# Masked attention with layer norm on one core: the layer norm's steps reordered on VectorE and GpSimd

## What is computed

```python
q = x @ Wq.T; k = x @ Wk.T; v = x @ Wv.T
rel = adj.T * (q @ k.T)                 # 1024 x 1024, mask of zeros and ones
rel = rel / norm(rel, axis=2)           # over the last axis, without the batch
y = x + rel @ v
out = (y - mean(y)) / sqrt(var(y) + 1e-5)
```

## Time and profile before

| | |
|---|---|
| median of 3 runs | 2031.97 us (2030.19 to 2032.34) |
| the profiled execution's own time | 2032.82 us |
| its span, first to last instruction | 2030.8 us |
| busy: PE, DVE, ACT, POOL | 97%, 75%, 35%, 47% |
| granted TensorE clock, mean | 0.994 of full speed |

### The profile page before, as it was taken

The page is one execution under the profiler, slowest core; times in us unless marked ns, Lnnn a source line. Parts: engine busy times, 40 slices in busy tenths (PEclk is TensorE's granted clock), DMA queues, the critical chain, the costliest instruction groups (busy, mean ns, idle before and its releaser), DMA issues.

```text
span 2030.8 us, 28664 instructions
## 1 busy us (share of the span) xinstructions
PE 1960.9 (97%) x9840; PEld 1667.5 (82%) x9840; DVE 1523.6 (75%) x2339; ACT 709.3 (35%) x1032; POOL 944.9 (47%) x640
## 2 busy tenths in 40 slices
PE   7799999999999999999999999999999999999998
PEld 5688878888787887878878788887888878788787
DVE  7587777877778777786877768777787777867776
ACT  5242424334243342323423234242433423334231
POOL 6543447344363443645534464343734436344352
PEclk8899999999999999999999999999999999999999
DMA  6534333344342434334352333543334434343411
GB/s 209 216 151 181 146 116 142 128 170 155 124 155 114 176 139 155 119 129 160 139 191 101 132 139 150 181 153 107 149 127 169 152 124 155 117 172 139 159 52 62
DMA packets 80414, 292.21 MB, mean 144 GB/s; under 512 B 7440, under 2 KB 7440, under 8 KB 76304
## 3 DMA queue, kind: packets, MB, share of 16 engines
q1 hardware_dynamic: 80400, 292.06, 39.0%
HBM read 251.13 MB, written 40.89 MB: 144 GB/s over the span
## 4 chain that ended last, share of the span: by engine, by line
PE 50%; issue 26%; POOL 17%; DVE 5%; DMA 1%; ACT 1%; POOLq 0%; DVEq 0%; SPq 0%; ACTq 0%
PE banks L410 17%; PE banks L412 17%; PE banks L411 17%; POOL square_sum L1057 8%; POOL scr L995 2%; POOL scr L987 2%; DVE x_lo L720 2%; POOL rstd L1074 2%; POOL rel L1050 1%; DMA w_kept<-v_raw 1%; POOL rnorm L1070 1%; DVE yv L887 1%; DVE stats L915 1%; DVE res L912 1%; DVE rel L823 1%
## 5 line engine op out<-in xcount | busy, mean ns | idle before, releaser
L410 PE MATMUL banks<-yv 128*128 128x512 f32 x1024 | 402.1, 393 | 38.9 <-DVE yv L887 38.9
L411 PE MATMUL banks<-yv 128*128 128x512 f32 x1024 | 399.0, 390 | 0.0
L412 PE MATMUL banks<-yv 128*128 128x512 f32 x1024 | 398.5, 389 | 0.0
L1057 POOL TENSOR_TENSOR square_sum<-square_sum,squares 128x512 f32<-128x512 f32 x224 | 319.8, 1428 | 87.2 <-ACT squares L639 76.6
L410 PE MATMUL banks<-yv,x_hi 128*128 128x512 f32 x896 | 349.7, 390 | 10.7 <-ACT rel L627 10.7
L411 PE MATMUL banks<-yv,x_hi 128*128 128x512 f32 x896 | 349.5, 390 | 0.0
L412 PE MATMUL banks<-yv,x_lo 128*128 128x512 f32 x896 | 349.5, 390 | 0.0
L1074 POOL TENSOR_TENSOR rstd<-var_eps,minus_half 128x1 f32<-128x1 f32 x128 | 130.4, 1018 | 316.0 <-DVE var_eps L919 316.0
L410 PEld LDWEIGHTS banks<-yv 128*128 128x128 f32 x1024 | 192.2, 188 | 90.4 <-DVE yv L887 51.6
L412 PE MATMUL banks<-aw,x_lo 128*128 128x256 f32 x896 | 253.6, 283 | 0.0
L411 PE MATMUL banks<-aw,x_hi 128*128 128x256 f32 x896 | 253.6, 283 | 0.0
(11 more groups left out here) (99 smaller groups left out, 3557.5 us busy)
## 6 DMA issues: line engine op xcount, KB each, us to landing
scr<-adj SPq DMA_DIRECT2D x128, 512.0 KB, 5.8
aw<-w_kept SPq DMA_DIRECT2D x16, 3584.0 KB, 11.0
aw<-a_kept SPq DMA_DIRECT2D x15, 3584.0 KB, 10.9
scr<-xT SPq DMA_DIRECT2D x32, 1024.0 KB, 7.1
res<-x SPq DMA_DIRECT2D x128, 256.0 KB, 2.7
out<-res SPq DMA_DIRECT2D x128, 256.0 KB, 2.0
a_kept<-aw SPq DMA_DIRECT2D x1, 3584.0 KB, 16.1
w_kept<-v_raw SPq DMA_DIRECT2D x3, 512.0 KB, 16.8
```

The source lines that it names most:

```text
L410: pe.matmul(bank_ap, l_hi, r_hi, start=first and i == 0, stop=False, skip_group_check=on)
L411: pe.matmul(bank_ap, l_hi, r_lo, start=False, stop=False, skip_group_check=on)
L412: mm = pe.matmul(bank_ap, l_lo, r_hi, start=False, stop=i == len(pairs) - 1, skip_group_check=on)
L1057: pool.tensor_tensor(square_sum[:, h, :], square_sum[:, h, :], squares[:, n % SQRING, :], ALU.add).then_inc(square_added, 1)
```

## The change

The reference to pieces by tile becomes a table, X_IN_TILE. On ScalarE the order of the instructions is the same as before (the loop is only written otherwise). On VectorE the x splits that belong to tile t+1 now stand behind the chunk's split in turn t, and ahead of `normalise(b, t)`; before, they stood behind it. Those of tile 0 still stand ahead of `output(b, 0)`. On GpSimd the power of tile t now stands ahead of the sum, and one sum follows each of the first four powers: power 0, S1, power 1, S3, power 2, S2, power 3, S4, powers 4 to 7. The last batch is as before. SP's and TensorE's programs are as before.

```diff
+        X_IN_TILE = {0: (X22,), 1: (X11, X12), 2: (S1,), 3: (S3,), 4: (S2,), 5: (S4,)}
...
                 norms(b)
                 for t in range(MT):
-                    if not last:
-                        for q in {0: (X22,), 1: (X11, X12), 2: (S1,), 3: (S3,), 4: (S2,), 5: (S4,)}.get(t, ()):
+                    if t == 0 and not last:
+                        for q in X_IN_TILE[0]:
                             x_piece(b + 1, q)
                     output(b, t)
                     if t + CRING < MT:
                         chunk(b, t + CRING)
+                    if not last:
+                        for q in X_IN_TILE.get(t + 1, ()):
+                            x_piece(b + 1, q)
                     normalise(b, t)
...
                 power_norm(b)
-                if not last:
-                    x_sum_of(b + 1, S1)
-                    x_sum_of(b + 1, S3)
-                power_var(b, 0)
-                if not last:
-                    x_sum_of(b + 1, S2)
-                power_var(b, 1)
-                if not last:
-                    x_sum_of(b + 1, S4)
-                for t in range(2, MT):
+                sums = {} if last else {0: (S1,), 1: (S3,), 2: (S2,), 3: (S4,)}
+                for t in range(MT):
                     power_var(b, t)
+                    for q in sums.get(t, ()):
+                        x_sum_of(b + 1, q)
```

More of the change, by code:

```diff
@@ L698, in batch @@
                         v_hi_piece(b, block, i)
+                if not last:
+                    for q in X_IN_TILE[0]:
+                        x_piece(b + 1, q)
                 for t in range(MT):
-                    if not last:
-                        for q in {0: (X22,), 1: (X11, X12), 2: (S1,), 3: (S3,), 4: (S2,), 5: (S4,)}.get(t, ()):
-                            x_piece(b + 1, q)
                     if t + CRING < MT:
                         chunk(b, t + CRING)
+                    if not last:
+                        for q in X_IN_TILE.get(t + 1, ()):
+                            x_piece(b + 1, q)
             y_first(0)
```

## The result

The changed kernel takes 2039.87 us (median of 6 runs, 2038.13 to 2040.39), the kernel before 2032.15 us beside it. The ratio is 1.0038, interval 1.0025 to 1.0051: slower by 7.7 us (0.4%), a quarter of the 29.7 us forecast.

What follows compares the result with a forecast made beforehand. TensorE, busy 97%, was taken as the bound, its waits for VectorE's chunk splits the winnable part. Later splits add 1.98 us a batch, 15 batches +29.7 us, to 2032.8: 2062.5 us, range 2048 to 2080.

Steps and rivals of the forecast that it cites:

- sign: Whole kernel: slower, by 29.7 us; slower was given 0.81, faster 0.15, no change 0.04.
- place: TensorE waits for VectorE's chunk splits at tiles 4 to 7, 0.34 us late, then 1.47 each.
- main mechanism: Each of four sums on GpSimd goes in ahead of VectorE's norm step and costs VectorE a full 2.26 us.
- the order of turns: VectorE and GpSimd: neither keeps its place from one instruction to the next; the one that stood goes in.
- the power's hold: Behind the chunk's split, VectorE's x split stands 0.40 us for GpSimd's power, four times a batch.
- the pace: VectorE, tiles 1 to 3: 7.02 us from chunk split to chunk split, against TensorE's 5.44.
- TensorE's waits: TensorE waits for the chunk's split 60 times, tiles 4 to 7, some 4.1 us of listed idle a batch.
- First rival: The norm step goes in ahead of the sum, no tile waits: faster, 1986 us; chance 0.15.
- second: Rival: only three of four sums hold VectorE, about 2029 us, next to no change; chance 0.04.
- third: Rival: the chunk's split stands too, or lateness reaches the next batch's products: 2078 us and up; chance 0.06.
- The rest: ScalarE's waits for sums, SP's later stores, x for tiles 5 to 7 and later line 775, costed at nothing.

Runs made afterwards that it cites:

- experiment 1: The kernel before with only GpSimd's order taken from the changed kernel (each sum right behind a power): 2068.74 us, ratio 1.0183.
- experiment 3: The changed kernel with each sum for the next batch cut to 2 of 512 columns, same instructions and waits: 1983.41 us, ratio 0.9767.
- experiment 4: The changed kernel with one wait more, GpSimd's sum after power t waiting for norm step t: 1983.80 us, ratio 0.9765.
- experiment 6: The changed kernel with each of the four sums split into two instructions of 512 columns: 1985.17 us, ratio 0.9764.
- experiment 2: The changed kernel with GpSimd's old order, so VectorE's part of the change alone: 2042.71 us, ratio 1.0054.
- experiment 7: The changed kernel with a tile's power over 8 columns in place of 1, the other 7 unused: 2059.2 us in one run.

## Why the prediction was wrong

- **Its sign, its place and its main mechanism were right.** Sums go in ahead of norm steps of 2.62 us (forecast 2.64) in tiles 1 to 3, X12's split stands for S1, and lines 912 to 919 run after the sum where they could have run beside it. Experiments 1, 3, 4 and 6 show it by four different times, each within 3 us of the time or range expected before it ran (1, 4 and 6 by the order of turns, 3 by the sums' length alone). Those expectations were written with the result and its trace at hand, and so with a power that holds nothing.
- **The term that failed is the power's hold**, in the prediction "the x split that is next on VectorE stands those 0.40 us. The wait is renamed, and I count its gain as nothing". The trace after, experiment 2's pace of 4.57 us and experiment 7 show that it stands for 0. With 1.22 - 0.08 in place of 0.40 + 1.08 the pace is 7.02 - 0.34 = 6.68 (measured 6.64), and tile 0 is 0.34 shorter too. Four times that is 1.4 us a batch, with 0.04 more in each of three tiles 1.5: 22 of the 22.6 us between forecast and result. The term counts four times a batch, and the forecast effect, 1.98 us a batch, was itself the difference between four sums' hold and what VectorE had lost and had in slack before; so this small term was three quarters of it.
- **What led to it:** from the power's row I knew when it ended after the chunk's split, 0.40, and read that as the time that it holds the ports. The row shows the first and not the second, and "splits and norm steps on VectorE never run together with a sum or a power" went beyond the rows: for a power they had only the power itself standing. No row of before had an instruction of VectorE standing behind a power, so the hold was unknown from 0 to 0.40, 24 us in all; I named that bound and took half of it into the range. In full it would have been 2062.5 - 24 = 2038.5, 1.4 us from the result.
- **TensorE's waits:** forecast 60, tiles 4 to 7; they were 45. At tile 4 the chunk was in time by then but for 0.1 us, which is the same 0.34 again.
- **First rival** (1986, the norm step ahead): it didn't happen by itself, but its price was right; experiment 4 brings it about and takes 1983.8. The second and third had no part.
- **The rest held.** ScalarE, the stores, x of the later tiles and line 775 cost nothing: in the list of waits after, TensorE has none that repeats but the 45 for the chunk's split.

## What to carry to other kernels

- Where VectorE and GpSimd share work in fp32, ask of each long GpSimd instruction what VectorE does while it runs: beside steps that read a bank, or one tensor in statistics, it was free, and ahead of a two-tensor or norm step it cost its whole length. One wait that put it there took 56 us from the changed kernel (2039.87 to 1983.80) and left it 48 us, 2.4%, under the kernel before.
- A short instruction that an engine is waiting for should go ahead of a long one only if the long one then doesn't go in ahead of its consumer: the consumer of the power stood for the sum that had been moved behind the power.
- The time at which an instruction ends after a release isn't the time that it holds a resource. If no row shows someone standing behind it, the range takes the whole bound.

## What the runs showed of the hardware

- The exclusion is not always for a whole GpSimd instruction. The Trainium skill, "SBUF — State Buffer", section "SBUF: two separate sides", says that whoever starts first has the pair of ports for the whole instruction. For the 128 x 1024 sums beside splits and norm steps the traces agree (a norm step of 2.62 in place of 0.54, a sum of 3.03 in place of 2.40). For the power they don't: an x split took its full-speed 1.22 us beside one that worked until 1.50 us after the chunk's split had let it in. A power does stand for a chunk split in front of it, though, 1.45 in place of 0.54.
- Turns alternate by instruction here: neither engine kept the ports for its next instruction while the other stood (experiment 6: sum half, norm step, sum half).
- Of a sum and a norm step that wait for the same power, the sum began 0.06 us earlier (experiments 1 and 7), and that made the norm step 2.60 or 2.61 us in place of 0.54.
